# Two attention layers on one core: second pass one place later in layer 0, causal masks of layer 1 on VectorE, token copies and sums on GpSimd

## The chip, the core and the metric

The kernel runs on one core of a Trainium2 chip, in one launch. The metric is the device time in microseconds of that core. Of the kernel before, three runs took 998.69, 994.81 and 999.81 us (median 998.69). A further execution was profiled.

## What is computed

The input is x of 16 batches by 256 tokens by 128 features, f32. Two blocks follow each other, and each computes x + s * g from the normalised tokens xn.

```python
xn = layernorm(x)
# block 0
s = attention(xn)        # 16 heads of 8; q, k, v = xn @ w_qkv + b_qkv
                         # scores = q k / sqrt(8) + relative position bias, softmax, @ v, @ w_out + b_out
g = silu(experts(xn))    # 8 experts, the best 2 of each token, weighted
x = x + s * g
# block 1
xn = layernorm(x)
scores = where(causal, q k / sqrt(8), lowest)
new = resid_gain * softmax(scores) + skip_gain * eye - centre_gain * uniform
s = (new @ v) @ cproj_w  # uniform[t, u] = 1 / (t + 1) for u <= t; the gains are per head
g = silu(xn @ W.T + b + (xn @ V_r) @ C.T)
x = x + s * g
```

## The kernel before, in words

The program has five parts in order: the setup (layer norm, router, bias tables, up to about 80 us of the span), the attention of layer 0 (to 462 us), the experts and the middle part (second layer norm, the gate of block 1; to about 700 us), and the attention of layer 1 (to the end). Each engine has a program of its own; they meet in semaphores.

**A step.** `attention` runs for both layers. Step k works on five batches at once: it projects q and k of batch k+2, loads the stacks of k+1, makes the first pass (kind A) of batch k, the second pass (kind B) and the first values of batch k-1, the last values, output copy and sums of k-2, and the output product of k-3. There are 16 batches, so steps -2 to 18 of layer 0 and -1 to 18 of layer 1 (its first projections lie in the middle part).

**Two passes.** The scores are needed with their row maximum taken off. q and k are split into three bf16 parts (`parts_one`, `rest_one`, `parts_two`, `rest_two`), stored to DRAM and read back as stacks. The first pass (`first_pass`, L1511 to L1524) computes scores with queries on the partitions, and VectorE takes the maxima (L1272). Their three bf16 parts (`maximum_parts` on VectorE or `parts_gpsimd`, L1216 to L1222) are transposed by TensorE at the end of the step (the turn, L1624), copied by ScalarE (`max_rows`, L1415) and written into rows 96 to 98 of the stack by a DMA (`maxima`, L1160). The second pass (`second_pass`, L1539 to L1550) computes the scores again, keys on the partitions, with the maximum subtracted by three more rows, and waits for that DMA. ScalarE's exponential follows, then the product with the values (`values`, L1567), which also makes the sums.

**Units and ring.** A pass has 8 units of 4 heads in layer 0 (each 128x1024 f32, two PSUM banks). In layer 1 it has 6: four with 4 heads and 256 columns, which contain a diagonal block, and two with 8 heads and 128 columns. The units of both passes go through a ring of three slots in an order that `Units` writes out: A0 A1 A2 B0 A3 B1 A4 B2 ... and the last three B. TensorE may fill a slot when the unit three places before it has been read. Every engine walks the same order, and constants put the other work at a place of it: `LATE`, `VALUES` (values), `SCALE`, `INVERT`, `PROJECT`, and literal places such as pos == 1 for the projections.

**Who reads a slot.** A-units are read by VectorE. In layer 0 the position bias of the first pass is added by TensorE from a table (L1511) and that of the second by VectorE (`add_bias`, L1282), which writes to SBUF, before the exponential (L1423). From step 3 (`HELP`) on, the units in `ASIDE` (0, 2, 4) are copied to SBUF by ScalarE (`take`, L1435) and get the bias from GpSimd (`bias_aside`, L1230), which from then on also does the rests and the parts of the maxima. Before step 3 VectorE does all of it. In layer 1 the causal masks are added by TensorE: for a 4-head unit two 256-wide matmuls of an identity and `maskB` (L1543) in the second pass, likewise `maskA` in the first. The exponential reads the slot directly (L1428).

**GpSimd at the start of layer 0.** Its program starts with 64 indirect stores that sort the tokens by expert into DRAM (L1239 to L1243), in two groups of 32 with a wait for the landings behind each, and only then takes up its first step.

**The rest of a step.** ScalarE copies the batch's tokens to xb (L1452) as its first work; the values' projection (`V`, L1597) reads xb. PSUM bank 7 (`misc`) is used in turn by QK, V, E (layer 1), Y and the turn. The outputs and sums go from PSUM to `ev` (L1441), to DRAM (`outputs_out`), back as `raw` and `rec`, VectorE inverts the sums (L1289), and they go out and back once more as `rden`. VectorE multiplies raw by rden (`scale`, L1298 in layer 0, with the gain L1300 in layer 1). In layer 1 TensorE makes two products for skip and centre (L1603, L1604), VectorE the running sum of the second (L1308), its scaling by 1/(t+1) (L1311) and two additions (L1309, L1313); then the output product (Y, L1613), gate (L1344) and residual (L1346). SP issues the DMAs in the order stacks, parts 0, outputs out, parts 1, sums and outputs in, parts 2, inverses out and in, maxima.

```python
def emit(eng, body):
    pipeline(eng, body, -1 if layer else -2, LOOP, 3, B + 2, 3, B)
```

Of the kernel before, what the change touches and what calls it, by code (L numbers as in the profile page):

```python
# [21 lines left out]
ALU = mybir.AluOpType  # L22
# [75 lines left out]
def build(nc, x_in, w_qkv, b_qkv, w_out, b_out, w1_rpe, b1_rpe, w2_rpe, b2_rpe, router_w, router_b,  # L98
          gu_w, gu_b, down_w, down_b, qk_w, qk_b, v_w, cproj_w, resid, skip, centre, f_w, f_b, f_v, f_c,
          consts, rel, out):  # L100
    with ExitStack() as ctx:
# [39 lines left out]
        v.wv1 = sb("wv1", [P, 2, P])  # L141
# [57 lines left out]
def setup(nc, v):  # L199
# [19 lines left out]
    rows = take(6 * P, 1).rearrange("p (a b) -> p a b", b=P)  # L219
    rowsp = take(6 * P, 1).rearrange("p (a b) -> p a b", b=P)  # L220
# [39 lines left out]
    with nc.Block() as block:  # L260
        def small_weights(dve):
# [5 lines left out]
            nc.vector.tensor_copy(v.cols[:, 4:6], ps[:, 2, 4:6]).then_inc(small_cp, 1)  # L267
# [80 lines left out]
        def _(sp):  # L348
# [13 lines left out]
            for dst, src in rpe:  # L362
# [4 lines left out]
                (v.wv1[:, 0, :], v.v_w[:, :]),  # L367
# [49 lines left out]
        def _(dve):  # L417
# [30 lines left out]
            for a in (0, 1, 3, 4):  # L448
# [4 lines left out]
                                  gains[0:1, 0, :].unsqueeze(2).broadcast_to([1, H, HD])).then_inc(copied, 1)  # L453
            nc.vector.tensor_copy(v.wv0[:], wqkv[:, 2 * P:3 * P]).then_inc(copied, 1)
            vw = v.wv1[:, 0, :].rearrange("p (h d) -> p h d", d=HD)
            nc.vector.tensor_tensor(v.wvs[:].rearrange("p (h d) -> p h d", d=HD), vw,
                                    gains[:, 1, :].unsqueeze(2).broadcast_to([P, H, HD]), ALU.mult).then_inc(copied, 1)
            nc.vector.scalar_tensor_tensor(v.wv1[:, 1, :].rearrange("p (h d) -> p h d", d=HD), vw, -1.0,
                                           gains[:, 2, :].unsqueeze(2).broadcast_to([P, H, HD]),
                                           ALU.mult, ALU.mult).then_inc(copied, 1)  # L460
# [37 lines left out]
        def _(pe):  # L498
# [30 lines left out]
            for k in range(6):  # L529
                nc.tensor.matmul(ps[:, 2, k:k + 1], rowsp[:, k, :], v.ones[0:1, 0:1], start=True, stop=True)  # L530
# [242 lines left out]
def middle(nc, v, before):  # L773
# [37 lines left out]
    def gpsimd(pool):  # L811
# [15 lines left out]
        pool.wait_ge(cleared, 3)  # L827
# [131 lines left out]
class Units:  # L959
# [3 lines left out]
    def __init__(self, count):  # L963
        self.count = count
        self.order = [("A", 0), ("A", 1), ("A", 2)]
        for j in range(count - 3):
            self.order += [("B", j), ("A", j + 3)]
        self.order += [("B", j) for j in range(count - 3, count)]
# [19 lines left out]
def attention(nc, v, layer, ahead_of=None):  # L988


    U = Units(8 if layer == 0 else 6)
# [33 lines left out]
    if layer == 0:  # L1025
        sorted_in = sem("sorted_in")
        labelled = sem("labelled")
    else:
        e_full, e_evac, shaped = sem("e_full"), sem("e_evac"), sem("shaped")
        fin_done = sem("fin")  # L1030
# [58 lines left out]
    with nc.Block() as block:  # L1089
        @block.sync  # L1090
        def _(sp):
# [71 lines left out]
            def body(s):  # L1163
                if s.has(1):
                    stacks(s)
                if s.has(2):
                    parts(s, 0)
                if s.has(-2):
                    outputs_out(s)
                if s.has(2):  # L1170
                    parts(s, 1)
                if s.has(-2):
                    sums_in(s)
                    outputs_in(s)
                if s.has(2):
                    parts(s, 2)
                if s.has(-2):
                    inverses_out(s)
                    inverses_in(s)
                if s.has():  # L1180
                    maxima(s)

            if layer:
# [3 lines left out]
                sp.wait_ge(v.cleared, 4)  # L1187
# [45 lines left out]
        def _(pool):  # L1233
# [13 lines left out]

            def body(s):
                if s.has(2) and (layer or s.k >= HELP):
                    rest_one(pool, nc.gpsimd, s)  # L1250
                for n, j in enumerate(apart(s.k)):
                    if n == 1 and s.has(2):
                        rest_two(pool, nc.gpsimd, s)
                    if s.has(-1):
# [3 lines left out]
                if layer == 0 and s.has() and s.k >= HELP:  # L1258
                    parts_gpsimd(pool, s)

            if layer:
                ahead_of[1](pool)
                pool.wait_ge(v.cleared, 4)
                body(first)
            emit(pool, body)

        @block.vector
        def _(dve):
# [22 lines left out]
            def scale(s):  # L1291
# [5 lines left out]
                if layer == 0:  # L1297
                    nc.vector.tensor_tensor(on[:], raw[:], rden[:], ALU.mult).then_inc(on_done, 1)  # L1298
                else:
                    nc.vector.scalar_tensor_tensor(on[:], raw[:], cols[:, 5:6], rden[:], ALU.mult, ALU.mult  # L1300
                                                   ).then_inc(on_done, 1)

            def add_shape(s):

                dve.wait_ge(e_full, s.n(-3) + 1)
                dve.wait_ge(on_done, s.n(-3) + 1)
                n = 2 * s.n(-3)
                nc.vector.tensor_tensor_scan(cum[:], v.onesT[:], misc[:, T:2 * T], 0.0, ALU.mult, ALU.add).then_inc(e_evac, 1)  # L1308
                nc.vector.tensor_tensor(on[:], misc[:, 0:T], on[:], ALU.add).then_inc(e_evac, 1)  # L1309
                dve.wait_ge(e_evac, n + 2)  # L1310
                nc.vector.tensor_tensor(cum[:], cum[:], v.share, ALU.mult).then_inc(shaped, 1)  # L1311
                dve.wait_ge(shaped, n + 1)
                nc.vector.tensor_tensor(on[:], on[:], cum[:], ALU.add).then_inc(shaped, 1)  # L1313
# [369 lines left out]
```

## Time and profile before

| | us |
|---|---|
| median of three runs (lowest, highest) | 998.69 (994.81, 999.81) |
| the profiled execution's own time | 1001.72 |
| its span, first to last instruction | 999.9 |
| TensorE, VectorE, ScalarE, GpSimd busy | 786, 646, 509, 411 |
| mean granted TensorE clock | 0.93 of full speed |

All instants are microseconds from the start of the span. PE is TensorE, PEld its weight loads, DVE VectorE, ACT ScalarE, POOL GpSimd, SP the queue that issues DMAs. L12 is line 12 of the kernel. Busy shares are means over stages with different limits. The ends of matmuls are modelled and overlap, so the starts of successive instructions say more than durations do. A bracket at the end of a timeline row gives the idle time before it and what released it.

### The profile page before, as it was taken

How to read it: one execution, taken by the hardware profiler on the slowest of the kernel's cores; microseconds unless marked ns; L12 is line 12 of the kernel's file. 1: busy time of each engine (PE TensorE's matmuls, PEld its weight loads, DVE VectorE, ACT ScalarE, POOL GpSimd, SP SyncE). 2: the span in 40 equal slices, each digit the busy share in tenths (PEclk: the TensorE clock that was granted, in tenths of full speed). 3: DMA queues.
4: the chain of work that ended last, by engine and by line, in shares of the span. 5: the costliest groups of instructions: out<-in, count | busy, mean ns of one | idle time of the engine just before them, and what ended most of it. 6: DMA issues, size and time to landing. Idle time of an engine off the chain costs nothing.

```text
span 999.9 us, 19881 instructions
## 1 busy us (share of the span) xinstructions
PE 786.2 (79%) x6259; PEld 506.5 (51%) x6278; DVE 645.5 (65%) x1137; ACT 509.3 (51%) x883; POOL 411.4 (41%) x394
## 2 busy tenths in 40 slices
PE   0894787989988998854999999525598898989984
PEld 0652444555554554422555555314476666666663
DVE  6552786887788778832655655366356767676763
ACT  1243254676677766642433433258365555555542
POOL 7006776554555454421777777673210101010000
PEclk9996899999999999986999999856799999999997
DMA  5595745444544453142212222240665646464621
GB/s 141 194 192 138 174 121 123 97 94 102 123 115 92 100 122 88 31 136 59 58 53 53 58 55 54 78 122 16 142 135 124 148 117 159 115 157 117 136 58 51
DMA packets 132671, 106.13 MB, mean 106 GB/s; under 512 B 23317, under 2 KB 124633, under 8 KB 129545
## 3 DMA queue, kind: packets, MB, share of 16 engines
q1 hardware_dynamic: 122348, 91.23, 39.8%
q0 software_dynamic: 4352, 8.99, 2.9%
q10 hardware_dynamic: 5920, 5.24, 1.7%
q8 instruction: 31, 0.51, 0.2%
q14 instruction: 20, 0.16, 0.1%
HBM read 54.60 MB, written 50.03 MB: 105 GB/s over the span
## 4 chain that ended last, share of the span: by engine, by line
PE 27%; DMA 10%; DVE 7%; issue 4%; ACT 4%; SPq 2%; POOL 1%; DVEq 0%; ACTq 0%; POOLq 0%
PE ps L671 8%; DMA od_d<-ev 5%; PE ps L692 3%; PE ps L1567 3%; DVE mx L1272 3%; DMA rec<-od_d 2%; PE ps L683 2%; PE ps L665 2%; PE ps L1576 1%; ACT rows L893 1%; PE ps L673 1%; PE ps L1519 1%; SPq L1113 1%; PE ps L1517 1%; PE ps L1545 1%
## 5 line engine op out<-in xcount | busy, mean ns | idle before, releaser
L1272 DVE TENSOR_REDUCE mx<-ps 128x4 f32<-128x1024 f32 (+1 forms) x224 | 268.4, 1212 | 146.8 <-PE ps L1513 69.9
L1423 ACT ACTIVATE probs<-probs 128x1024 f32<-128x1024 f32 x128 | 131.8, 1051 | 64.9 <-DVE probs L1282 63.6
L1428 ACT ACTIVATE probs<-ps 128x1024 f32<-128x1024 f32 x96 | 96.8, 1024 | 82.9 <-PE ps L1545 55.8
L1202 POOL TENSOR_TENSOR qkr<-qkf,qk 128x512 f32<-128x512 f32 x27 | 31.3, 1160 | 244.0 <-ACT qk L1392 238.4
L1230 POOL TENSOR_TENSOR probs<-probs,tabB 128x1024 f32<-128x1024 f32 x42 | 99.5, 2369 | 74.6 <-ACT probs L1435 74.6
L1511 PE MATMUL ps<-tabA,eyeb 128*128 128x512 bf16 x256 | 102.3, 399 | 25.9 <-DMA ks<-parts_d 10.9
L1567 PE MATMUL ps<-probs,vpad 128*32 128x256 f32 (+1 forms) x2048 | 118.7, 362 | 4.2 <-ACT probs L1423 3.6
L1282 DVE TENSOR_TENSOR probs<-ps,tabB 128x1024 f32<-128x1024 f32 x86 | 101.5, 1210 | 4.3 <-PE ps L1539 4.3
L1513 PE MATMUL ps<-ks,qs 96*128 96x256 bf16 x512 | 102.3, 282 | 0.0
L1539 PE MATMUL ps<-qs,ks 99*128 99x256 bf16 x512 | 77.2, 280 | 6.8 <-DMA qs<-mT 2.6
L671 PE MATMUL ps<-qs,probs 128*128 x144 | 80.9, 644 | 1.4
L762 POOL TENSOR_TENSOR probs<-probs 128x256 f32<-128x256 f32 x72 | 53.5, 743 | 67.2 <-ACT probs L718 58.0
L730 DVE TENSOR_SCALAR probs<-ps 128x256 f32<-128x256 f32 x72 | 30.6, 425 | 73.1 <-PE ps L673 50.4
L765 POOL DMA_INDIRECT mixed<-probs x72 | 72.7, 1010 | 12.0 <-issue 11.7
L1567 PEld LDWEIGHTS ps<-probs,vpad 128*32 128x32 f32 x2048 | 55.8, 110 | 42.8 <-issue 16.9
L712 ACT ACTIVATE probs<-ps 128x256 f32<-128x256 f32 x72 | 27.7, 385 | 87.8 <-PE ps L683 87.8
L1513 PEld LDWEIGHTS ps<-ks,qs 96*128 96x128 bf16 x512 | 52.2, 102 | 38.4 <-issue 5.5
L1243 POOL DMA_INDIRECT slots_in<-rows,place x64 | 62.8, 981 | 19.6 <-issue 18.9
L1539 PEld LDWEIGHTS ps<-qs,ks 99*128 99x128 bf16 x512 | 44.5, 99 | 38.6 <-DVE mx L1272 15.3
L1435 ACT ACTIVATE probs<-ps 128x1024 f32<-128x1024 f32 x42 | 42.5, 1013 | 29.8 <-PE ps L1539 29.8
L1543 PE MATMUL ps<-maskB,eyeb 128*128 128x256 bf16 x128 | 35.1, 275 | 17.0 <-DVE mx L1272 14.2
L1511 PEld LDWEIGHTS ps<-tabA,eyeb 128*128 128x128 bf16 x256 | 25.6, 100 | 43.7 <-DVE probs L1282 18.7
(226 smaller groups left out, 1530.1 us busy)
## 6 DMA issues: line engine op xcount, KB each, us to landing
parts_d<-qk SPq DMA_DIRECT2D x64, 192.0 KB, 4.3
qs<-parts_d SPq DMA_DIRECT2D x32, 384.0 KB, 5.0
ks<-parts_d SPq DMA_DIRECT2D x32, 384.0 KB, 6.7
parts_d<-qk SPq DMA_DIRECT2D x64, 128.0 KB, 3.2
od_d<-ev SPq DMA_DIRECT2D x64, 128.0 KB
slots_in<-probs SPq DMA_DIRECT2D x1, 4680.0 KB
probs<-slots_in SPq DMA_DIRECT2D x72, 65.0 KB, 1.8
parts_d<-qk SPq DMA_DIRECT2D x64, 64.0 KB, 1.9
```

Of the source, the lines that this page charges most:

```text
L671: nc.tensor.matmul(ps[:, b, :], xgT[:, b, :], wgu[:, bass.ds(e, 1), :].rearrange("p a n -> p (a n)"), start=True, stop=False)
L765: nc.gpsimd.indirect_dma_start(v.mixed[:, :], bass.IndirectOffsetOnAxis(ap=rows[:, b:b + 1], axis=0), yo[:, b % 4, :], None).then_inc(y_st ...
L1230: nc.gpsimd.tensor_tensor(p, p, v.tabB[:, heads[0]:heads[0] + 4, off:off + T], ALU.add).then_inc(biased, 1)
L1243: nc.gpsimd.indirect_dma_start(v.slots_in[:, :], bass.IndirectOffsetOnAxis(ap=v.place[:, k, t:t + 1], axis=0), v.rows[:, t, :], None).then ...
L1272: nc.vector.tensor_reduce(mx[:, s.buf(), t, heads[0]:heads[-1] + 1], ring[:, slot].rearrange("p (h n) -> p h n", n=w), AX.X, ALU.max).then ...
L1282: nc.vector.tensor_tensor(probs[:, j, :].rearrange("p (h n) -> p h n", n=T), ring[:, slot].rearrange("p (h n) -> p h n", n=T), v.tabB[:, h ...
L1423: nc.scalar.activation(probs[:, j, :], probs[:, j, :], ACT.Exp).then_inc(exp_done, 1)
L1428: nc.scalar.activation(probs[:, j, :], ring[:, slot], ACT.Exp).then_inc(exp_done, 1)
L1511: nc.tensor.matmul(o[:, T * n:T * n + 2 * T], eyeb[:], v.tabA[:, h:h + 2, off:off + T], start=True, stop=False, skip_group_check=True)
L1513: mm = nc.tensor.matmul(at, q, ks[0:MROW, b, h, :], start=False, stop=True, skip_group_check=True)
L1539: mm = nc.tensor.matmul(at, k, qs[0:MROW + PARTS, b, h, :], start=(n % 2 == 0), stop=True, skip_group_check=True)
L1567: mm = nc.tensor.matmul(od[32 * q:32 * q + 32, T * (i % 2) + t0:T * (i % 2) + T], vpad[:, b, 4 * c + q, at:at + 32], probs[:, j, w * n:w * ...
```

## The change

The core of the diff; what is left out are the same moves written for the other layer or engine, and names.

```diff
-    def __init__(self, count):
+    def __init__(self, count, lead):
...
-        self.order = [("A", 0), ("A", 1), ("A", 2)]
-        for j in range(count - 3):
-            self.order += [("B", j), ("A", j + 3)]
+        self.order = [("A", j) for j in range(lead)]
+        for j in range(count - lead):
+            self.order += [("B", j), ("A", j + lead)]
...
-    U = Units(8 if layer == 0 else 6)
+    U = Units(8, 4) if layer == 0 else Units(6, 3)
...
-    LATE = 2 if layer else 4
-    SCALE = 2 if layer else 0
-    INVERT = 7 if layer else 10
-    VALUES = {9: (0, 1)} if layer else {13: (0, 1), 15: (2, 3)}
-    ASIDE = () if layer else (0, 2, 4)
-    ORDER = tuple(range(NU)) if layer else (1, 0, 3, 2, 5, 6, 4, 7)
-    PROJECT = 10 if layer else 8
+    LATE = {2: (2, 3), 4: (4, 5)} if layer else {3: (2, 3), 6: (4, 5), 8: (6, 7)}
+    VALUES = {8: (0, 1)} if layer else {12: (0, 1)}
+    SCALE, INVERT, PROJECT = (None, 11, 10) if layer else (7, 15, 10)
+    QK, V, TURN = (3, 5, 11) if layer else (3, 5, 14)
+    ASIDE = () if layer else (0, 2, 3)
+    ORDER = tuple(range(NU)) if layer else (1, 0, 2, 4, 5, 6, 3, 7)
+    A_PART, A_OUT, A_TWO, A_VAL, A_MAX = (3, 4, 4, 5, 10) if layer else (4, 7, 5, 5, 12)
+    SEQ = ((("take", 0),), (("exp", 1),), (("take", 2), ("exp", 0)), (("take", 3), ("exp", 2)), (("exp", 4),),
+           (("exp", 5),), (("exp", 6), ("exp", 3)), (("exp", 7),))
```

`LATE` gives the places of the values of batch k-2, `QK`, `V` and `TURN` those of the projections and of the turn on TensorE, the `A_` names those of ScalarE's work, `SEQ` what ScalarE does at each second-pass unit of layer 0. In SP's order, layer 0 now has parts 0, 1, 2, then outputs out, sums and outputs in, maxima, inverses; layer 1 stacks, parts 0, outputs out, parts 1, 2, sums and outputs in, maxima, inverses.

GpSimd, in both layers; the 64 indirect stores of layer 0 stay in front of its first step:

```diff
+            def tokens(s):
+
+                if s.has(-1):
+                    pool.wait_ge(v_full, s.n(-1) + 1)
+                nc.gpsimd.tensor_copy(xb[:], xnT[:, bass.ds(s.n() * T, T)]).then_inc(xb_done, 1)
...
+            def running_mean(s):
+
+                pool.wait_ge(e_evac, 2 * (s.n(-3) + 1))
+                nc.gpsimd.tensor_tensor(cum[:], cum[:], v.share, ALU.mult).then_inc(shaped, 1)
+                pool.wait_ge(shaped, 2 * s.n(-3) + 1)
+                nc.gpsimd.tensor_tensor(on[:], on[:], cum[:], ALU.add).then_inc(shaped, 1)
...
             def body(s):
+                if s.has():
+                    tokens(s)
                 if s.has(2) and (layer or s.k >= HELP):
                     rest_one(pool, nc.gpsimd, s)
                 for n, j in enumerate(apart(s.k)):
                     if n == 1 and s.has(2):
                         rest_two(pool, nc.gpsimd, s)
+                    if n == 2 and s.has():
+                        parts_gpsimd(pool, s)
                     if s.has(-1):
                         bias_aside(pool, s, n, j)
...
-                if layer == 0 and s.has() and s.k >= HELP:
-                    parts_gpsimd(pool, s)
```

In layer 1 GpSimd's step is: tokens, rest one, raw times rden, rest two, running mean, parts of the maxima, residual. The copy to xb on ScalarE, and on VectorE the multiply, the scaling and last addition, the parts and the residual of layer 1 are gone.

VectorE and TensorE in layer 1:

```diff
+            def causal(s, j, slot):
+
+                dve.wait_ge(full["B"], NU * s.n(-1) + j + 1)
+                diagonal = ring[:, slot].rearrange("p (h n) -> p h n", n=T)[:, :, 0:P]
+                nc.vector.tensor_tensor(diagonal, diagonal, maskB[:].unsqueeze(1).broadcast_to([P, 4, P]), ALU.add
+                                        ).then_inc(masked, 1)
...
-                nc.vector.tensor_tensor_scan(cum[:], v.onesT[:], misc[:, T:2 * T], 0.0, ALU.mult, ALU.add).then_inc(e_evac, 1)
-                nc.vector.tensor_tensor(on[:], misc[:, 0:T], on[:], ALU.add).then_inc(e_evac, 1)
+                nc.vector.tensor_tensor_scan(cum[:], v.onesT[:], misc[:, 0:T], 0.0, ALU.mult, ALU.add).then_inc(e_evac, 1)
                 dve.wait_ge(on_done, s.n(-3) + 1)
+                nc.vector.scalar_tensor_tensor(on[:], misc[:, 0:T], cols[:, 5:6], on[:], ALU.mult, ALU.add
+                                               ).then_inc(e_evac, 1)
...
-                        nc.tensor.matmul(misc[:, 0:T], v.wvs[:], batch_tokens(s, -3), start=True, stop=True)
-                        nc.tensor.matmul(misc[:, T:2 * T], v.wv1[:, 1, :], batch_tokens(s, -3), start=True, stop=True
-                                         ).then_inc(e_full, 1)
+                        nc.tensor.matmul(misc[:, 0:T], v.wv1[:], batch_tokens(s, -3), start=True, stop=True).then_inc(e_full, 1)
```

The gain of the softmax part is folded into the values' weights, the skip gain becomes a column used by VectorE, and the centre gain is multiplied into `share` once, by GpSimd, before layer 1. The exponentials of units 0 to 3 wait for the mask.

## Rows read from the trace of the kernel before

**Rows 1.** Windows over one step of each layer: length, busy time (instructions), clock, DMA share, GB/s.

```profile
204.20:224.20 20.00, 18.10 (x158) 10.47 (x158) 15.96 (x18) 14.16 (x21) 10.34 (x9) 1.00 0.49 110
839.60:856.20 16.60, 15.12 (x177) 11.30 (x173) 11.89 (x18) 9.55 (x16) 2.32 (x2) 1.00 0.60 138
```

**Rows 2.** Timeline of TensorE in one step of layer 0: start, duration, instruction.

```profile
286.58 1.12 PE L1576 MATMUL ps<-xnT,wqk 128*128 x4
287.54 0.38 PE L1511 MATMUL ps<-tabA,eyeb 128*128 128x512 bf16 x1
...
289.38 1.07 PE L1567 MATMUL ps<-probs,vpad 128*32 128x256 f32 x16
290.39 0.61 PE L1539 MATMUL ps<-qs,ks 99*128 99x256 bf16 x4
290.83 0.61 PE L1597 MATMUL ps<-wv,xb 128*128 128x128 f32 x4
291.28 0.38 PE L1511 MATMUL ps<-tabA,eyeb 128*128 128x512 bf16 x1
...
304.25 0.26 PE L1624 MATMUL ps<-eyeb,m 128*96 128x128 bf16 x1 [0.93 <-POOL m L1222]
```

**Rows 3.** Groups of instructions: line, shapes, count | busy, mean ns | idle before.

```profile
L1230 POOL TENSOR_TENSOR probs<-probs,tabB 128x1024 f32<-128x1024 f32 x42 | 99.5, 2369 | 74.6 <-ACT probs L1435 74.6
...
L1282 DVE TENSOR_TENSOR probs<-ps,tabB 128x1024 f32<-128x1024 f32 x86 | 101.5, 1210 | 4.3 <-PE ps L1539 4.3
...
L1543 PE MATMUL ps<-maskB,eyeb 128*128 128x256 bf16 x128 | 35.1, 275 | 17.0 <-DVE mx L1272 14.2
...
L1604 PE MATMUL ps<-xnT,wv 128*128 (+1 forms) x32 | 10.0, 394 | 0.0
...
L1339 DVE TENSOR_TENSOR rows<-ps,bo 128x256 f32 (+1 forms) x16 | 6.7, 416 | 3.6 <-PE ps L1613 3.6
```

**Rows 4.** Timeline of GpSimd around the 64 indirect stores.

```profile
123.68 0.24 POOL L1239 COPY rows<-rowid 128x32 f32<-128x32 f32 x1 [1.64 <-DMA slots_in<-rows,place]
...
163.86 0.97 POOL L1243 DMA_INDIRECT slots_in<-rows,place  x1 [0.30 <-issue]
170.40 1.15 POOL L1202 TENSOR_TENSOR qkr<-qkf,qk 128x512 f32<-128x512 f32 x1 [5.57 <-DMA slots_in<-rows,place]
```

**Rows 5.** Timeline of TensorE in step 0 of layer 0.

```profile
94.93 0.61 PE L1511 MATMUL ps<-tabA,eyeb 128*128 128x512 bf16 x1 [10.90 <-DMA ks<-parts_d]
...
100.52 0.61 PE L1597 MATMUL ps<-wv,xb 128*128 128x128 f32 x4
...
110.08 0.31 PE L1624 MATMUL ps<-eyeb,m 128*96 128x128 bf16 x1 [3.32 <-DVE m L1328]
```

**Rows 6.** Timeline of TensorE: the first instruction of steps 3, 4 and 15, layer 0.

```profile
156.98 0.38 PE L1511 MATMUL ps<-tabA,eyeb 128*128 128x512 bf16 x1 [0.31 <-DVE probs L1282]
...
184.42 0.39 PE L1511 MATMUL ps<-tabA,eyeb 128*128 128x512 bf16 x1
...
404.08 0.38 PE L1511 MATMUL ps<-tabA,eyeb 128*128 128x512 bf16 x1
```

**Rows 7.** Timelines of GpSimd, VectorE and TensorE in layer 1.

```profile
843.78 1.16 POOL L1202 TENSOR_TENSOR qkr<-qkf,qk 128x512 f32<-128x512 f32 x1 [13.46 <-ACT qk L1392]
...
843.92 1.29 DVE L1300 SCALAR_TENSOR_TENSOR on<-raw,cols,rden 128x256 f32<-128x256 f32 x1
...
846.41 0.28 PE L1543 MATMUL ps<-maskB,eyeb 128*128 128x256 bf16 x1 [1.23 <-DVE mx L1272]
...
943.46 0.48 DVE L1300 SCALAR_TENSOR_TENSOR on<-raw,cols,rden 128x256 f32<-128x256 f32 x1
```

**Rows 8.** Waits of the SP queue, 770 to 950: total us, times, longest.

```profile
SPq L1132 <- DMA od_d<-ev: 31.7, 11, 5.9
```

**Rows 9.** Timeline of TensorE: the first instruction of steps 3 and 15, layer 1.

```profile
755.77 0.28 PE L1517 MATMUL ps<-maskA,eyeb 128*128 128x256 bf16 x1
...
955.90 0.28 PE L1517 MATMUL ps<-maskA,eyeb 128*128 128x256 bf16 x1
```

More of the change, by code:

```diff
@@ L140, in build @@
         v.wv0 = sb("wv0", [P, P])
[L141 removed]
+        v.wv1 = sb("wv1", [P, P])
         v.wvs = sb("wvs", [P, P])
@@ L528, in _ @@
             pe.wait_ge(copied, 4 + 4 + 13)
-            for k in range(6):
+            for k in range(7):
                 nc.tensor.matmul(ps[:, 2, k:k + 1], rowsp[:, k, :], v.ones[0:1, 0:1], start=True, stop=True)
@@ L1165, in body @@
                     stacks(s)
[L1166 to L1181, printed above, removed]
+                if layer == 0:
+                    if s.has(2):
+                        parts(s, 0)
+                        parts(s, 1)
+                        parts(s, 2)
+                    if s.has(-2):
+                        outputs_out(s)
+                        sums_in(s)
+                        outputs_in(s)
+                    if s.has():
+                        maxima(s)
+                    if s.has(-2):
+                        inverses_out(s)
+                        inverses_in(s)
+                else:
+                    if s.has(2):
+                        parts(s, 0)
+                    if s.has(-2):
+                        outputs_out(s)
+                    if s.has(2):
+                        parts(s, 1)
+                        parts(s, 2)
+                    if s.has(-2):
+                        sums_in(s)
+                        outputs_in(s)
+                    if s.has():
+                        maxima(s)
+                    if s.has(-2):
+                        inverses_out(s)
+                        inverses_in(s)
             if layer:
@@ L1351, in body @@
                         scale(s)
+                    if layer and pos == 6 and s.has(-3):
+                        add_shape(s)
                     if U.exists(s.k, kind):
@@ L1356, in body @@
                             add_bias(s, j, U.slot(s.k, pos))
-                    if kind == "A" and j == NU - 1 and s.has() and (layer or s.k < HELP):
+                        elif layer and j < 4:
+                            causal(s, j, U.slot(s.k, pos))
+                    if kind == "A" and j == NU - 1 and s.has() and (layer == 0 and s.k < HELP):
                         maximum_parts(s)
-                    if layer and pos == 6 and s.has(-3):
-                        add_shape(s)
                     if pos == INVERT and s.has(-2):
@@ L1474, in body @@
                     act.dma_start(v.wdn, v.down_w.rearrange("e (c i) h -> i e c h", c=2)).then_inc(v.w_load, 16)
-                if s.has():
+                if A_MAX >= len(U.order) and s.has():
                     max_rows(s)
@@ L1615, in body @@
                         mm.then_inc(y_full, 1)
+                    if pos == TURN and s.has():
+                        turn_maxima(s)
                     if U.exists(s.k, kind):
```

151 lines of the change are left out of this document (80 added, 71 removed).

## Prediction

> **What bounds the kernel now.** I read first the windows laid over single steps. In the first layer a step of 20.0 us has TensorE busy for 18.1, VectorE for 16.0, ScalarE for 14.2 and GpSimd for 10.3 us; in the second a step of 16.6 us has 15.1, 11.9, 9.6 and 2.3 us [rows 1]. TensorE leads in both, and its modelled ends overlap, so next I read the starts of its instructions in one step [rows 2]: the projections take 0.96 us (286.58 to 287.54), a unit of the first pass 0.9 (two units from 287.54 to 289.38), two units of probabilities times values 1.0, a unit of the second pass 0.44, the values' projection 0.45. Eight first-pass units, eight second-pass units, eight value units, QK, V, the output product (as V) and the turn of 0.1 make 7.2 + 3.5 + 4.0 + 0.96 + 0.45 + 0.45 + 0.1 = 16.7 us of issue, so some 3.3 us of each 20 are waits. The longest single one is the turn of the maxima (304.25, 0.93 us before it, released by GpSimd's last part): GpSimd adds a bias of 2.37 us [rows 3] before it starts on the parts. Then the timeline of GpSimd at the start of layer 0, for what stands in front of its first step, and last layer 1 at the place where TensorE waits.
>
> **Part 1, the token copy on GpSimd: a new wait at the start.** ScalarE wrote xb before; now GpSimd does, in both layers. Nothing guards it for the first steps, and GpSimd's program for layer 0 opens with the 64 indirect stores. Their last is issued at 163.86 and GpSimd is free at 170.40, having waited 5.57 us for landings; after the first 32 it waited only 1.64 us [rows 4]. The values' projection of step 0 needs xb. It ran at 100.52 [rows 5]; now it waits until the stores have landed. Queued behind it on TensorE are first-pass units 4 to 7 of step 0, the turn, and all of step 1. With TensorE quiet nothing else moves data, so I take the short landing: 163.86 + 0.97 + 1.64 = 166.5, plus a 256-wide copy on GpSimd (between 0.24 us, its 32-wide copy, and 1.15, its 512-wide subtraction [rows 4]; 0.6, between them) = 167.2 us. Shift **+66.7 us** (with the long landing +70.6). V to turn took 9.6 us (100.52 to 110.08) with five units behind it; now four, but TensorE comes from idle: the 512-wide table matmul after an idle of 10.9 us took 0.61 us against 0.38 in a warm step [rows 2, 5], which is the 1.2 GHz level against 2.4. I leave 9.6.
>
> Steps 1 and 2 were 46.8 us (from the turn at 110.08 [rows 5], with 0.1 for it, to 156.98 [rows 6]), and VectorE does all 16 passes and the parts there: 16 at 1.14 us (a later step's 16.0 us less 1.2 for three small operations, over 13 [rows 1]), plus 2.3 for rest and parts, 20.5 us, plus 1.2 idle at the start of a step. I take 43.5 for both, **-3.3 us**. Step 3 took 27.4 us (156.98 to 184.42), because GpSimd was not free before 170.4; that wait has moved to step 0, so step 3 becomes an ordinary one of 18.3, **-9.1 us**. At 184.42 the changed kernel is behind by 66.7 - 3.3 - 9.1 = **54.3 us**.
>
> **Part 2, the order of layer 0.** The ring still has three slots, so the fourth first-pass unit waits for the first one's maximum; "four ahead" only moves the second pass one place back. VectorE's work does not change. I laid the new order out by hand with the durations above, a unit being readable 1.08 us (first pass) or 0.65 us (second) after its start, and 0.06 us back. Marks from the first unit of a step: A0 0; A1 1.0 and A2 2.2, each behind a bias add of the step before; values 2, 3 at 3.0; QK 4.0; A3 5.0; B0 5.9; V 6.3; A4 6.7; values 4, 5 at 7.6; B1 8.6; A5 9.1; values 6, 7 at 9.9; B2 10.9; A6 11.4; Y 12.2; B3 12.7; A7 13.1; B4 14.0; values 0, 1 at 14.4; B5 15.4; the turn at 16.8, since A7's maximum ends at 15.4 and the parts take 1.3; B6 17.0; B7 17.4; next A0 17.8. GpSimd's parts now stand before its third bias, so a whole 2.37 us add leaves the path of the turn, and the maxima reach the second pass two units later in PE's order, which hides their landing. I take 18.3 for small losses the layout misses. Steps 4 to 15 took (404.08 - 184.42)/11 = 19.97 us [rows 6]: 12 x 1.67 = **-20.0 us**. The last step of second passes alone waits for the turned maxima; the earlier turn gives **-1.5**.
>
> The multiply of raw and rden stays on VectorE in layer 0, but at place 7, where GpSimd is busy with a bias or the rest. In layer 1 the same operation took 1.29 us while GpSimd's subtraction, started 0.14 us earlier, ran for 1.16, and 0.48 us when GpSimd was idle [rows 7]. I charge nothing, because VectorE idles 0.5 us before A6 and again before A7; uncovered it is 0.8 us a step.
> The Trainium skill, page "SBUF — State Buffer", section "SBUF: two separate sides", says that a VectorE operation with two SBUF inputs and a GpSimd operation that reads SBUF take one port pair under an exclusive lock, whichever starts first. By that rule, the trace agrees (1.29 against 0.48 us), and the multiply could wait out a whole bias add; with that the sum would be some 12 us higher.
>
> **Part 3, layer 1.** TensorE loses the eight mask matmuls of second-pass units 0 to 3: 128 of them in the layer [rows 3], as wide as the four matmuls that make a second-pass unit of 0.44 us [rows 2], so 0.11 us of issue each and 0.88 us a step; and one of two 256-wide f32 products, 0.44 us (32 instructions for it in the layer [rows 3], two per product, each 0.22 by the rate of V, whose four are half as wide). Its issue in a step was 14.9 us (16.6 less the 1.23 us wait at 846.41 [rows 7] and 0.5 in small waits) and becomes 13.6. That wait is for a maximum held up behind the colliding multiply; with the multiply on GpSimd nothing on VectorE has two SBUF inputs, so that wait goes too. Added to VectorE: four masks over 128x512 in PSUM. Between 0.42 us (128x256 from PSUM with an SBUF operand) and 1.21 (128x1024) [rows 3]; on the line through both it is 0.68. Four cost 2.7 us; the multiply, two adds, cum, and the four small parts leave (about 3.9), so VectorE's load hardly moves. But a mask stands between TensorE and ScalarE: unit 1 of the second pass is masked behind A3's maximum, its exponential ends near 9.0 us into the step, and A5 needs that slot at 8.6. Laid out as before: A0 0, B0 4.0, A3 5.3, B1 6.4, A4 7.3, A5 9.1, B4 11.9, turn 13.2, B5 13.4, next A0 14.3. GpSimd's work (about 6 us) fits.
> What is late next is the output's chain. ScalarE copies it at place 4 now, so its stores leave SP at some 7.3 instead of 5.2 us, and SP has waited up to 5.9 us for them to land [rows 8]; then the sums, and the inverse on VectorE at place 11, ahead of the next step's first maximum. It should be ready at 15.5, where that maximum could start at 15.1. SP's later maxima then land as B0 needs them. For both I add 0.6: 14.9 us. Steps took (955.90 - 755.77)/12 = 16.68 us [rows 9]: 13 x 1.78 = -23.1, and -2.5 for steps 1 and 2, **-25.6 us**. At the end one pass is shorter by the masks and three additions run slower on GpSimd: **-1.0**. The weights' preparation adds one small multiply: nothing, since it lies before the tables' turn.
>
> **Sum.** 54.3 - 20.0 - 1.5 - 25.6 - 1.0 = **+6.2 us**. The profiled execution took 1001.7 us (span 999.9), so 1007.9; it stands 3.0 above the median of 998.7, against which I forecast **1005 us**.
>
> **Rivals.** (a) The steps reach TensorE's sums nearly: 17.2 and 14.0 us. Then 54.3 - 12 x 2.77 - 1.5 - (13 x 2.68 + 2.5) - 1.0 = -19: **980 us**, faster. For it: both layouts give less than I took (17.8 and 14.3). Against: the stores' shift does not shrink. It decides if both steps are below 18.0 and 14.6. (b) Waits take the gains' place: masks queue behind maxima and the inverse holds VectorE, 16.0 and 19.3 us. Then 54.3 - 8.0 - 1.5 - (8.8 + 1.5) - 1.0 = +33: **1032 us**. For it: second-pass slots come free later and the output's stores wait up to 5.9 us today. (c) The lock: the multiply of layer 0 comes behind bias adds and its 0.8 us is on the path, 15 times: +12 on the forecast, **1017 us**. (d) The change does not do what I read: the copy is not held by the stores. Then the 66.7 falls away and step 3 still waits for GpSimd: -66.7 + 9.1 on the forecast, **947 us**. Against: GpSimd took up its first step only at 170.40 [rows 4].
>
> **How the numbers follow.** The forecast's own range is 995 to 1015 (steps off by 0.3 us over 27 steps, the landing 0 or 4 us): 0.44. (a) 0.27, (b) 0.17, (c) 0.09, (d) 0.03. The bound for a difference that can be told is 0.5%, 993.7 to 1003.7. Below it lie (d) and nearly all of (a): 0.29; between, the lower part of the forecast and a rest of (a): 0.22; above 0.49. Both signs have much of the chance, so the range is wide: 983 to 1028 leaves out (d) and the far halves of (a) and (b).
>
> **What would show it.** GpSimd's first copy of tokens after its last indirect store, near 167 us, and TensorE idle for some 65 us before it: if the values' projection of step 0 still runs near 100 us, the main term is wrong. Step 3 like step 4; steps near 18.3 and 14.9 us; the turn's wait near 0.9 us; no multiply over 1 us in layer 1; a mask near 0.68 us. If the inverse on VectorE waits over 1 us in most steps of layer 1, it is (b).

## The result, and the profile after

The changed kernel took **1066.1 us** (median of four runs, 1063.6 to 1070.1), the kernel before 999.0 us in the same session: a ratio of 1.068, with a 95% interval of 1.064 to 1.073. The forecast was 1005 us, with a range of 983 to 1028. The profiled execution took 1063.6 us; its span is 1061.8 us against 999.9.

The turn of the maxima runs once per step on TensorE and is a good mark. Its rows in the timeline of TensorE of the changed kernel, for steps 0, 3 and 15 of layer 0 and 0, 2 and 15 of layer 1:

```profile
174.36 0.31 PE L1640 MATMUL ps<-eyeb,m 128*96 128x128 bf16 x1 [3.09 <-DVE m L1392]
...
235.94 0.23 PE L1640 MATMUL ps<-eyeb,m 128*96 128x128 bf16 x1 [0.75 <-POOL m L1240]
...
452.91 0.23 PE L1640 MATMUL ps<-eyeb,m 128*96 128x128 bf16 x1 [0.75 <-POOL m L1240]
...
756.54 0.23 PE L1640 MATMUL ps<-eyeb,m 128*96 128x128 bf16 x1 [2.97 <-POOL m L1240]
...
784.82 0.23 PE L1640 MATMUL ps<-eyeb,m 128*96 128x128 bf16 x1 [0.30 <-POOL m L1240]
...
1023.16 0.23 PE L1640 MATMUL ps<-eyeb,m 128*96 128x128 bf16 x1
```

The same marks in the trace of before stand at 110.08 [rows 5], 184.05, 423.09, 724.02, 753.73 and 969.00. Laid against the terms of the forecast they split the difference of 61.9 us of span:

| stretch, by turns | before | after | difference | forecast |
|---|---|---|---|---|
| start to turn 0, layer 0 | 110.1 | 174.4 | **+64.3** | +66.7 |
| steps 1 to 3 | 74.0 | 61.6 | **-12.4** | -12.4 |
| steps 4 to 15 | 239.0 | 217.0 | **-22.1** | -20.0 |
| turn 15 of layer 0 to turn 0 of layer 1 | 300.9 | 303.6 | **+2.7** | -1.5 |
| steps 1 to 15, layer 1 | 245.0 | 266.6 | **+21.6** | -25.6 |
| last turn to the end | 30.9 | 38.6 | **+7.7** | -1.0 |

The changed kernel makes the turn before the last one or two second-pass units of its step, where the kernel before made it behind all of them. For that reason alone a stretch that ends with turn 3 or 15 is 0.6 to 0.9 us shorter in the table, and the next one longer by as much (behind turn 3 the first instruction of step 4 starts 0.94 us later in the changed kernel, at 236.88, and 0.37 before).

Layer 0 came out as reckoned. The error lies in layer 1, 47 of its 56 us within the steps.

The windows over one step of layer 0 and two successive ones of layer 1 answer to [rows 1] (length, busy time and instructions of PE, PEld, DVE, ACT, POOL, clock, DMA share, GB/s):

```profile
310.50:328.75 18.25, 17.41 (x158) 10.57 (x157) 16.79 (x17) 13.86 (x20) 10.65 (x11) 1.00 0.52 119
893.55:912.88 19.33, 16.73 (x161) 11.49 (x160) 11.51 (x15) 8.74 (x15) 6.51 (x11) 0.82 0.50 118
912.88:931.08 18.20, 15.59 (x163) 10.73 (x160) 11.57 (x15) 8.84 (x15) 6.52 (x11) 0.91 0.54 126
```

A step of layer 0 went from 20.0 to 18.25 us. A step of layer 1 went from 16.6 to 18.3 us (mean of steps 3 to 15). In the middle of the stage steps of 19.3 and 18.2 us alternate, as the two shown do, 18.8 on average. That is so although TensorE issues fewer matmuls and no other engine has more than 11.6 us of work. The clock column shows something new: 0.82 and 0.91 in the middle of a busy stage.

Of TensorE's waits inside such a step one stands out. Its timeline, with the step's first instruction and then from the second pass's unit 1 on:

```profile
894.56 0.27 PE L1580 MATMUL ps<-maskA,eyeb 128*128 128x256 bf16 x1
...
901.18 0.60 PE L1602 MATMUL ps<-qs,ks 99*128 99x256 bf16 x4
904.39 1.22 PE L1661 MATMUL ps<-xnT,wv 128*128 x2 [2.60 <-ACT vpad L1470]
905.40 0.63 PE L1585 MATMUL ps<-maskA,eyeb 128*128 128x512 bf16 x1
...
909.24 0.63 PE L1587 MATMUL ps<-ks,qs 96*128 96x128 bf16 x4
...
911.97 0.38 PE L1605 MATMUL ps<-maskB,eyeb 128*128 128x512 bf16 x1
```

L1661 is the product for skip and centre, E. It writes PSUM bank 7, which the values' projection V holds until ScalarE has copied it to `vpad`. TensorE stands still for 2.60 us, and then the 512-wide matmuls take 0.63 us instead of 0.38: from 904.39 on it ran at the 1.2 GHz level, and was back at 2.4 by 911.97. The wait alone does not bring the low level about each time: the first two steps with E waited as long and kept the full clock, as step 4 shows:

```profile
812.34 0.69 PE L1661 MATMUL ps<-xnT,wv 128*128 x2 [2.61 <-ACT vpad L1470]
812.87 0.38 PE L1585 MATMUL ps<-maskA,eyeb 128*128 128x512 bf16 x1
```

These two steps took 16.7 and 16.9 us, against 18.8 for the later ones. ScalarE's timeline shows what V's copy stands behind:

```profile
901.59 0.63 ACT L1459 ACTIVATE qk<-qkr 128x512 bf16<-128x512 f32 x1
902.88 1.02 ACT L1494 ACTIVATE probs<-ps 128x1024 f32<-128x1024 f32 x1 [0.66 <-DVE ps L1376]
903.80 0.44 ACT L1470 ACTIVATE vpad<-ps 128x128 f32<-128x128 f32 x2
```

And VectorE's shows what that exponential waited for, a maximum and then a mask:

```profile
900.94 1.23 DVE L1335 TENSOR_REDUCE mx<-ps 128x4 f32<-128x1024 f32 x1 [1.08 <-PE ps L1582]
902.08 0.69 DVE L1376 TENSOR_TENSOR ps<-ps,maskB 128x512 f32<-128x512 f32 x1
```

So the chain is: first-pass unit 3, its maximum, the mask of second-pass unit 1, its exponential, V's copy, E. The last two are in this order because the change moved V's copy in layer 1 from place 4 to place 5 (`A_VAL`), where it comes after the exponential. V itself moved with it on TensorE, from place 4 to 5. Before, the copy came at place 4, ahead of that exponential, and no product E waited for it. The waits over 840 to 990 show that this happens in each of the eight steps there (total us, times, longest):

```profile
DVE cum L1367 <- PE ps L1661: 22.4, 8, 3.0
PE ps L1661 <- ACT vpad L1470: 20.6, 8, 2.6
```

At the start of the kernel, the timeline of GpSimd:

```profile
161.71 0.96 POOL L1261 DMA_INDIRECT slots_in<-rows,place  x1 [0.31 <-issue]
164.05 0.40 POOL L1270 COPY xb<-xnT 128x256 f32<-128x256 f32 x1 [1.39 <-DMA slots_in<-rows,place]
```

and that of TensorE, with V of step 0 behind it:

```profile
164.59 1.19 PE L1655 MATMUL ps<-wv,xb 128*128 128x128 f32 x4 [63.98 <-POOL xb L1270]
```

### The profile page after: what moved, and what is told of

Same layout as the page of the kernel before. It is cut to its first block, busy times and chain, and to the rows that moved or that the text cites. A ratio compares the mean times of both kernels' runs of the same rounds, so it can differ in the third digit from the quotient of the medians.

```text
span 1061.8 us, 19652 instructions
## 1 busy us (share of the span) xinstructions
PE 781.7 (74%) x6101; PEld 497.1 (47%) x6120; DVE 652.8 (61%) x1073; ACT 493.2 (46%) x851; POOL 483.9 (46%) x555
## 4 chain that ended last, share of the span: by engine, by line
PE 33%; issue 6%; DVE 4%; ACT 4%; DMA 3%; POOL 2%; SPq 0%; POOLq 0%; ACTq 0%; DVEq 0%
PE ps L671 7%; PE ps L1624 4%; PE ps L692 3%; PE ps L1582 2%; PE ps L1602 2%; DVE mx L1335 2%; PE ps L1585 2%; PE ps L683 2%; PE ps L1587 2%; PE ps L665 1%; PE ps L1580 1%; ACT rows L894 1%; PE ps L1661 1%; PE ps L1633 1%; PE ps L673 1%
## 5 line engine op out<-in xcount | busy, mean ns | idle before, releaser
L1494 ACT ACTIVATE probs<-ps 128x1024 f32<-128x1024 f32 x96 | 96.4, 1021 | 107.5 <-DVE ps L1376 107.2
L1624 PE MATMUL ps<-probs,vpad 128*32 128x256 f32 (+1 forms) x2048 | 125.3, 369 | 7.1 <-ACT probs L1486 6.7
L1602 PE MATMUL ps<-qs,ks 99*128 99x256 bf16 x768 | 119.5, 283 | 5.1 <-DMA qs<-mT 3.4
L1602 PEld LDWEIGHTS ps<-qs,ks 99*128 99x128 bf16 x768 | 69.0, 101 | 45.0 <-issue 24.9
L1655 PE MATMUL ps<-wv,xb 128*128 128x128 f32 x64 | 10.4, 287 | 64.0 <-POOL xb L1270 64.0
L1448 ACT ACTIVATE qkf<-ps,cols 128x256 f32<-128x256 f32 x32 | 15.2, 474 | 83.4 <-PE ps L1633 82.5
L1376 DVE TENSOR_TENSOR ps<-ps,maskB 128x512 f32<-128x512 f32 x64 | 44.4, 694 | 13.1 <-PE ps L1602 12.0
```

Source lines behind the costliest of these rows:

```text
L1494: nc.scalar.activation(probs[:, j, :], ring[:, slot], ACT.Exp).then_inc(exp_done, 1)
L1602: mm = nc.tensor.matmul(at, k, qs[0:MROW + PARTS, b, h, :], start=(n % 2 == 0), stop=True, skip_group_check=True)
L1624: mm = nc.tensor.matmul(od[32 * q:32 * q + 32, T * (i % 2) + t0:T * (i % 2) + T], vpad[:, b, 4 * c + q, at:at + 32], probs[:, j, w * n:w * ...
```

## The experiments

**Run 1, V's copy before the exponential.** The theory from the trace: the place of V's copy costs the steps of layer 1. The edit, in ScalarE's loop over the places:

```diff
                     if pos == A_OUT and s.has(-2):
                         outputs(s)
+                    if layer and pos == A_VAL and s.has():
+                        values(s)
                     if kind == "B" and U.exists(s.k, kind):
...
-                    if pos == A_VAL and s.has():
+                    if layer == 0 and pos == A_VAL and s.has():
                         values(s)
```

> Theory A (the bank): in layer 1 the skip-and-centre product waits 2.6 us for ScalarE to empty V out of PSUM bank 7, and that copy stands behind the exponential of unit 1, which waits for its mask; the idle TensorE then drops to half clock. With V emptied ahead of that exponential the wait goes, the clock stays at 1.0 and steps 3 to 15 fall from 18.7 to 14.6 us: 13 x 4.1 = 54, so about 1012 us. Theory B (the masks): what paces layer 1 is that second-pass units pass through VectorE before ScalarE; then the steps stay above 18 and the time within 10 us of 1066.

Measured: 1024.0 us, ratio to before 1.026 (1.023 to 1.030), so **42 us** less than the changed kernel. Steps went from 18.8 to 15.2 us. In windows over a step and in TensorE's timeline of this run:

```profile
863.63:878.86 15.23, 14.08 (x160) 9.91 (x160) 11.15 (x14) 8.78 (x15) 6.47 (x12) 1.00 0.64 152
```

```profile
887.97 0.69 PE L1663 MATMUL ps<-xnT,wv 128*128 x2 [0.91 <-ACT vpad L1470]
888.50 0.38 PE L1587 MATMUL ps<-maskA,eyeb 128*128 128x512 bf16 x1
```

E still waits 0.91 us, but the clock stays at 1.00. That is theory A's cause and not its whole size: it had said 1012 us and steps of 14.6, because it let the whole wait go. Of the 3.5 us per step that went, 1.4 are idle time (2.6 to 1.2, length less busy) and 2.1 are busy time (16.2 to 14.1 on average): the same work at the full clock. Steps 3 and 4 of the changed kernel, 16.7 and 16.9 us with the wait and without the low clock, split it in the same way.

**Run 2, the masks of the second pass back on TensorE**, and nothing else:

```diff
-                        elif layer and j < 4:
-                            causal(s, j, U.slot(s.k, pos))
...
-                    if j < 4:
-                        act.wait_ge(masked, 4 * s.n(-1) + j + 1)
...
+                    elif w == T:
+                        if n % 2 == 0:
+                            diagonal = o[:, T * n:T * n + 2 * T].rearrange("p (h t) -> p h t", t=T)[:, :, 0:P]
+                            nc.tensor.matmul(diagonal, eyeb[:], maskB[:].unsqueeze(1).broadcast_to([P, 2, P]),
+                                             start=True, stop=False, skip_group_check=True)
```

> Theory A: the exponential of unit 1 starts only some 0.7 us earlier without a mask, so the product's wait shrinks from 2.6 to about 1.9 us, and TensorE has 0.88 us of masks more: the step stays at 18.7 within 0.5, the time at 1066 within 6. Theory B: with the masks off VectorE the steps return to 16.7 or less, so 1040 us or less.

Measured: 1036.2 us, ratio 1.037 (1.033 to 1.041), 30 us less. The theory I held, that V's place alone explains the time, missed here by 30 us. The time and the steps, 16.4 us, are those that theory B named. Its reason, that the masks pace every second-pass unit, does not hold by itself, since run 1 left all masks on VectorE and has shorter steps (15.2 us). A mask costs as a link of the chain in front of V's copy. With it gone, E's wait is 1.54 us instead of 2.60, and after the shorter wait the clock did not fall, in this or any other step from step 2 on:

```profile
894.48 0.69 PE L1662 MATMUL ps<-xnT,wv 128*128 x2 [1.54 <-ACT vpad L1468]
895.01 0.38 PE L1580 MATMUL ps<-maskA,eyeb 128*128 128x512 bf16 x1
```

**Run 3, the token copies of layer 0 on ScalarE again.**

```diff
             def body(s):
-                if s.has():
-                    tokens(s)
...
+                if layer == 0 and s.has():
+                    if s.has(-1):
+                        act.wait_ge(v_full, s.n(-1) + 1)
+                    nc.scalar.activation(xb[:], xnT[:, bass.ds(s.n() * T, T)], ACT.Copy).then_inc(xb_done, 1)
```

> Layer 0's token copies on ScalarE as before, layer 1's stay on GpSimd. Theory C (start): the 64.3 us that the first turn came late go, but GpSimd is again busy until 170 when step 3 needs it, which costs about 8 us: 1066 - 64 + 8 = 1010 us. Rival: the stores were also in the way of steps 1 and 2, which then go back to 23 us each (now 19.9 and 22.2): 1014 us.

Measured: 1008.4 us, ratio 1.010 (1.006 to 1.013), 58 us less: theory C. Turn 0 is at 108.6, V of step 0 at 100.65. Steps 1 and 2 take 20.1 and 21.0 us, so the rival's 23 did not come. Step 3 is long again, 26.98 us from turn to turn against 19.52: GpSimd takes up its work only after the stores.

```profile
162.96 0.96 POOL L1261 DMA_INDIRECT slots_in<-rows,place  x1 [0.30 <-issue]
167.14 1.15 POOL L1220 TENSOR_TENSOR qkr<-qkf,qk 128x512 f32<-128x512 f32 x1 [3.22 <-DMA slots_in<-rows,place]
```

**Run 4, the last step of layer 1 without GpSimd.** The end of the changed kernel had grown by 7.7 us. GpSimd's last work, and then its queue's own last instruction in the view of a source line (duration min, median and max in ns, first and last start):

```profile
1054.92 0.72 POOL L1291 TENSOR_TENSOR yt<-x,yt 128x256 f32<-128x256 f32 x1 [1.88 <-DVE yt L1407]
```

```profile
L1093 POOLq DRAIN  x2: 6730/7472/8213, 467.5 to 1054.9; - x2
```

The last output store is issued at 1055.67, and the span ends at 1061.8. The edit gives VectorE the four operations of GpSimd in the last step (two of them shown):

```diff
-                if s.has(-3):
+                if s.has(-3) and s.k < B + 2:
                     scale(s)
...
+                        if s.k == B + 2:
+                            nc.vector.tensor_tensor(cum[:], cum[:], v.share, ALU.mult).then_inc(shaped, 1)
+                            dve.wait_ge(shaped, 2 * s.n(-3) + 1)
+                            nc.vector.tensor_tensor(on[:], on[:], cum[:], ALU.add).then_inc(shaped, 1)
```

> The last step's four GpSimd operations (multiply, running mean, sum, residual) on VectorE. Theory D (drain): GpSimd's drain at the end takes 6.7 us and starts 5.6 us later than the last output store needs it; with GpSimd done early it is hidden and the end comes some 4 us after the last addition less: 4 from the drain and 1.2 from shorter operations, so 1061 us. Rival: the drain is a wait for the output's DMA, and nothing but the 1.2 us is won: 1065 us.

Measured: 1062.0 us, ratio 1.065 (1.061 to 1.068); the span is 1056.6, 5.2 shorter, and the last stretch fell from 38.6 to 34.2 us. The medians, 1066.1 and 1062.0, differ by less than the runs of either kernel scatter; the last stretch is the better measure. It is 38.4 to 39.4 us in the changed kernel and runs 1 to 3, without this edit, and 33.0 to 34.9 us in runs 4 to 8, with it. The drain is as long as before, but starts with GpSimd's last work in the step before the last, and 8.2 us later the kernel is still busy. So it was no wait for the output's DMA, as the rival had it. Of the 4.4 us, the shorter operations are some 1.2, an estimate from 0.72 us on GpSimd against 0.42 on VectorE for each of the four. The drain's row in this run:

```profile
L1093 POOLq DRAIN  x2: 6730/7470/8210, 466.7 to 1045.6; - x2
```

**Runs 5 to 7: all three repairs; with the masks on TensorE; with V one place earlier.** The fifth run joins the edits of 1, 3 and 4. The sixth adds that of 2. The seventh changes the fifth:

```diff
-    QK, V, TURN = (3, 5, 11) if layer else (3, 5, 14)
+    QK, V, TURN = (3, 4, 11) if layer else (3, 5, 14)
...
+                    if layer and pos == 4 and s.has():
+                        values(s)
                     if pos == A_OUT and s.has(-2):
                         outputs(s)
-                    if layer and pos == A_VAL and s.has():
-                        values(s)
```

> The changed kernel with all three edits of the first four runs: in the second layer ScalarE empties the token-to-value product before the exponential of unit 1, ScalarE makes the token copies of the first layer, and VectorE does the last step's four operations of GpSimd. Theory A with C and D (the three costs lie in three stretches and are independent, so that the measured savings add up): 1066.1 - 42 - 58 - 4 = 962 us, between 957 and 968; the first turn of the maxima near 108.6, 13 steps of the second layer near 15.2. Rival B (one saving was another's cover, as the two steps that were long behind the late start were): above 975 us. A result near 999 would mean that the change as written has nothing to gain over the kernel before even with its three faults gone.

Measured: **961.1 us**, ratio 0.963 (0.959 to 0.967). The three savings add up as theory A had them, to within 1 us.

> The same with the causal masks of the second layer's second pass put back on TensorE (sixteen matmuls with the identity in four units, two to a pair of heads, instead of four additions on VectorE). It prices the move of the masks once the wait for the values' bank is gone. Theory A (with the wait gone the step is what TensorE computes plus about 1 us, and eight matmuls of 256 columns at 0.11 us of start-to-start time are 0.9 us per step, 14 to 16 steps): 962 + 13 = 975 us. Rival B (the additions stand in the chain from product to exponential and delay the copy that frees the bank, as the run with the masks back and nothing else hinted): within 4 us of the run with three repairs, or below it.

Measured: 958.0 us, ratio 0.961 (0.958 to 0.965). Rival B: putting the masks back costs nothing, and 13 us were expected by theory A. The steps, fifth run first, then the sixth:

```profile
820.00:835.24 15.24, 14.09 (x160) 9.92 (x160) 11.21 (x14) 8.78 (x15) 6.49 (x12) 1.00 0.65 150
```

```profile
848.09:863.38 15.29, 14.82 (x170) 10.74 (x168) 9.00 (x10) 8.80 (x14) 6.52 (x11) 1.00 0.63 150
```

TensorE is busy 0.7 us longer and idle 0.7 us less. The step was not bound by its matmuls.

> The three repairs, and the second layer's token-to-value product one place earlier on TensorE (before the first pass's unit 3 instead of before the second pass's unit 1), with ScalarE emptying it as the first thing at that place, before the outputs' copy and the second part. The 0.9 to 1.0 us by which the skip-and-centre product still waits in each step goes. Theory A (that wait is what separates 15.2 us from what TensorE computes): steps near 14.3, and 962 - 14 = 948 us, 943 to 955. Rival B (the token-to-value product now waits itself, for the copy that empties the projections' bank one place before, 1 us or more): 960 us or above.

Measured: 958.3 us, ratio 0.961 (0.955 to 0.967), outside theory A's 943 to 955 and near rival B's number, but not by its cause. V did not wait; E's wait is gone, and two thirds of it came back at the ring. The waits over 800 to 930 and a step of the seventh run:

```profile
ACT probs L1502 <- DVE ps L1374: 39.5, 30, 3.9
...
PE ps L1599 <- ACT probs L1502: 5.7, 8, 0.9
```

```profile
850.68:865.60 14.92, 14.07 (x160) 9.92 (x160) 11.18 (x14) 8.78 (x15) 6.48 (x12) 1.00 0.66 155
```

Now a unit of the first pass waits 0.7 us for an exponential to free its slot, and the exponentials wait for masks.

**Run 8, V at place 4 and the masks on TensorE.**

> Three repairs, the token-to-value product at place 4, and the second pass's masks on TensorE again: the two variants that each gave about 958 us together. In the run with place 4 a second-layer step took 14.92 us of which TensorE was busy 14.07, and waited for a slot of the ring; with the masks on TensorE it was busy 14.8 of 15.29. Theory A (the additions on VectorE only lengthen the chain from product to exponential, and what TensorE saves by them it waits for a slot): the masks' 0.7 us fill the wait, steps stay between 14.8 and 15.0, and the time is that of the run with place 4, 955 to 960 us. Rival B (the masks' time on TensorE adds to the step): steps near 15.6, 13 x 0.7 = 9 us more, 967 us.

Measured: **955.3 us**, ratio 0.957 (0.954 to 0.960), theory A. A step of this run:

```profile
850.22:865.07 14.85, 14.82 (x170) 10.73 (x168) 8.72 (x10) 8.90 (x14) 6.52 (x11) 1.00 0.70 159
```

TensorE is busy all through the step: the masks fill the gaps that the slot left. This is the best of all the kernels here, 4.3% below the one before, though it and the sixth and seventh can't be told apart with certainty.

From turn 0 to turn 15 of layer 1, the runs make a small table of the two causes (runs 5 and 6 have other edits too, but outside this stretch):

| us | V's copy behind the exponential | V's copy before it |
|---|---|---|
| masks on VectorE | 266.6 (changed kernel) | 227.2 (run 5) |
| masks on TensorE | 238.6 (run 2) | 224.9 (run 6) |

The masks cost 28 us in the one column and 2 in the other; V's late copy costs 39 us in the one row and 14 in the other. Both together cost 26 us more than the two single costs add up to. Only in the one cell with both is the granted clock below 1.00 in any step from step 2 on, and there it costs some 2 us in each step from step 5 on.

## Why the prediction was wrong

**The start, right.** The largest term was +66.7 us for a token copy behind 64 indirect stores, measured +64.3. The landing took 1.39 us, near the short one of 1.64 that I chose, and the copy 0.40 instead of 0.6. The rest came with the last store, at 161.71 instead of 163.86. Run 3 shows the cause: with the copy on ScalarE 58 us go, not 64, since step 3 becomes long again by 7.5 us. That is the trade between the terms +66.7 and -9.1.

**Steps 1 to 3 of layer 0, right in the sum.** -3.3 and -9.1 make -12.4, and -12.4 was measured: steps 1 and 2 took 42.1 us, 1.4 less than I took, and step 3 took 19.5, 1.2 more. That the sum meets the forecast to 0.1 us is partly luck, since the two misses cancel and the mark's new place is worth 0.6 us.

**Layer 0's steps, right.** The layout gave 17.8, I took 18.3, and the trace shows 18.25. The turn's wait is 0.75 us in the rows above, where I had said near 0.9. The multiply at place 7 did collide, as one of its rows shows beside the row of GpSimd:

```profile
320.63 1.23 DVE L1360 TENSOR_TENSOR on<-raw,rden 128x256 f32<-128x256 f32 x1
```

```profile
320.41 1.17 POOL L1225 TENSOR_TENSOR qk<-qkr,qk 128x512 bf16<-128x512 f32 x1
```

It took 1.23 us beside a GpSimd operation of 1.17, and 0.42 at the shortest; 11 of the 16 took 1.13 to 1.24 us. The step took 18.25 us all the same, within the forecast that charged nothing, and rival (c)'s 12 us did not come about. No run takes the collision away. So a part of it may lie in the 0.45 us by which the step is longer than the layout, which I had allowed for as small losses.
The Trainium skill, page "SBUF — State Buffer", section "SBUF: two separate sides", has a VectorE operation with two SBUF inputs wait out the GpSimd operation that holds the shared ports. By that rule, the trace agrees (1.23 against 0.42 us).

**Layer 1's steps, the step that failed.** The term -25.6 was measured as +21.6. I laid out layer 1 "as before": marks for the ring's slots, the output's chain and the inverse, with 0.6 us for both. The layout followed slots and left out bank 7, which QK, V, E, Y and the turn use in turn. I had read that V's copy moves to place 5, and that unit 1's exponential is masked behind A3's maximum; I never asked who waits for what stands behind that exponential. I asked what is queued behind the added wait for the slot of A5 alone. The exponential itself came as laid out: it was to end near 9.0 us into the step and ended at 903.9, 9.3 us in. But the layout has A4 at 7.3 us and no mark for E, which stands in front of A4; E came at 9.8 us and A4 at 10.8 (904.39 and 905.40, with the step's start at 894.56). What the runs put in its place:
- E waits 2.6 us for V's copy (run 1: without that order -42 us).
- From step 5 on TensorE also drops to 1.2 GHz, for some 3 to 7 us of each step (granted clock 0.91 and 0.82), which I had not thought of at all; by run 1 that is 2.1 of the 3.5 us per step.
- Steps 1 and 2, in which E does not exist yet, took 14.22 and 14.06 us. They are lighter than the 14.9 us step of the forecast, since the output product is missing too and two value units in step 1, so they bear the layout out only roughly. Of the 2.5 us forecast for them 1.4 came (29.7 us before, 28.3 after); all of the rest of the miss lies in steps 3 to 15, +23.1 us instead of -23.1.
- With the chain repaired the steps take 15.2 us, and 14.9 with V one place earlier (runs 5 and 7). So the forecast's size held for a kernel without the fault, and only 0.3 us a step separates the fifth run from it. It did not hold term by term: the 0.88 us of mask matmuls gave nothing. Run 8 has them, is busy for 14.82 us and takes 14.85; what went there is idle time, 1.5 us of it in a step of the kernel before (16.60 less 15.12, [rows 1]).
The Trainium skill, page "Perfetto Trace Analysis", section "Matmuls", advises that independent groups of matmuls rotate through different PSUM banks, so that one's evacuation overlaps the next one's matmuls. The trace agrees: V and E share one bank, and E waited 2.60 us for an evacuation that the order of another engine had put late.

**The masks.** I reckoned 0.88 us a step of TensorE saved and 0.68 us per addition. An addition takes 0.694 us, and TensorE's busy time fell by 0.73 (14.82 to 14.09, runs 6 and 5). The error was to count the saving as time: run 8 has the masks on TensorE, is busy for the whole of 14.85 us, and is no slower than run 7.

**The ends.** From layer 0's last turn to layer 1's first I took -1.5 and it was +2.7, of which 0.6 to 0.9 us are the mark's new place. In the runs this stretch varies between 301.7 and 304.8 us without my having edited it; the cause is open. For layer 1's end I took -1.0, it was +7.7. I had counted three slower additions and not GpSimd's closing drain, hidden under VectorE's and TensorE's work before and exposed once GpSimd had work in the last step. Run 4 moves 4.4 us of it. Another 3.3 stay, of which some 0.8 are the mark's. The rest is not settled: in the last steps the outputs' copy comes behind late values that stand behind a wait for the maxima, and I did not try to move these.

**The rivals.** (b) named the right kind, waits taking the gains' place, at 1032 us. But its steps of 16.0 us are far from 18.3, and its sign, an inverse that waits over 1 us in most steps of layer 1, was not there: one step shows it, with 1.20 us. With the larger wait gone the sign appears. The inverse waits 1.5 to 2.7 us for the sums in most steps of run 1. In the step of run 1 whose E row stands above it ended at 880.31, and the maximum behind it then waited 0.39 us more for its own product, so it delayed nothing there. But in one step each of runs 1 and 5 the sums came late, and there rival (b)'s path is real. VectorE in run 5:

```profile
776.41 0.35 DVE L1350 RECIPROCAL rec<-rec 128x32 f32<-128x32 f32 x1 [4.66 <-DMA rec<-od_d]
```

Three maxima stand behind it, then the mask of unit 0, its exponential and V's copy, and E waited 2.15 us. That step took 17.25 us against 15.2, and the one of run 1, with 4.11 us, 16.71. Why these sums came late is open.

## What to carry to other kernels

When an operation gets a new wait, list what its engine has behind it in program order, and for each of these every buffer it frees, single-buffered PSUM banks first; moving one short copy ahead of one exponential was worth 42 us here. A wait of TensorE in mid-stage may cost twice: first its own length (16.8 us a step instead of 15.2 here), and then the work behind it at half the clock (18.8). Work taken off the leading engine is a gain only if that engine had no gap to put it in, which one run with the work put back shows at once.

## What the hardware showed that I had not expected

- In this stage the clock level fell after waits of 2.43 to 2.61 us and stayed at full after waits of 2.15 (one step of run 5), 1.54 and 0.91 us. The length of the wait does not decide it alone: the changed kernel kept the full level through its first two such waits, of 2.43 and 2.61 us, and run 4 through one of 2.60 between steps that lost it. Once the level fell not at the wait's end but 1 us after it (E at 998.22, first slow matmul at 999.22).
- GpSimd's drain at the end of a block took 6.7 and 8.2 us, here behind a last operation of 0.72 us. It cost nothing where the other engines still had that much to do: in the kernel before, the last one starts at 929.3 of 999.9 us.
- On GpSimd a 128x256 f32 addition or multiplication takes 0.73 us, and VectorE needs 0.42 for the same; in the steps this did not matter: GpSimd was busy for 6.5 of 18 us, and between 840 and 990 TensorE waited for nothing but V's copy.
